# Split expert weights in DRAM rows of 2 KB, and two scratch places for the activations of a transformer layer's expert stage

## The chip, the cores and the metric

One Trainium2 chip, one NeuronCore of it. The metric is the device time of one execution in microseconds, the median of several; the profile is one more execution. The five engines named below are TensorE (PE in the profile; PEld are its weight loads), VectorE (DVE), ScalarE (ACT), GpSimd (POOL) and SyncE (SP). SP, ACT and GpSimd also issue DMAs, each into a queue of its own: q1 is SP's, q10 ACT's, q0 GpSimd's. All queues are served by the same 16 DMA engines of the core.

## The reference

A layer with adaptive normalization on x of 2 x 4096 tokens and 512 channels. The first half is a linear attention, the second a mixture of 8 experts, of which each token takes 2:

```python
h = _layernorm(x) * (1 + ca) + sa
x = x + ga * _L0_attn_ref(h, w_qkv, w_proj, b_proj)
h = _layernorm(x) * (1 + cb) + sb
x = x + gb * _L0_ffn_ref(h, router_logits, gating_einsum, linear, per_expert_scale, router_scale)
# in _L0_ffn_ref, with the tokens sorted by expert:
gate_out = jax.lax.ragged_dot(sorted_xs, w_gate, group_sizes=tokens_per_expert)    # 512 -> 2 x 512
activation = jax.nn.gelu(gate_out[:, 0, :]) * gate_out[:, 1, :]
expert_outputs = jax.lax.ragged_dot(activation, linear, group_sizes=tokens_per_expert)  # 512 -> 512
```

The experts' sizes follow from the router and differ.

## The kernel before, in words

Every fp32 product is computed as three products of split operands: a = hi + lo, each rounded to fp32r, and hi x hi + hi x lo + lo x hi (PASSES).

**Attention stage, groups of 512 tokens, 16 groups.** Beside it the expert weights are split, since they are needed in that form later: SP loads them raw, ACT makes hi, DVE and GpSimd make lo, and SP stores both parts to a DRAM tensor, expert_split (`store_expert`, 64 stores of 768 KB, the only writes to it). An expert has 6144 weights per partition; they are kept as four quarters of QW = 1536, each as hi and lo. Before the change, a DRAM row of expert_split is one partition's hi and lo of one quarter, 3072 floats = 12 KB; a store writes half of it, 6 KB.

**Routing stage, 16 groups.** Projection, second norm, router, and a scatter of every token's row (528 floats) into the lists of its two experts in expert_rows, by indirect DMAs of GpSimd. Before its last group SP already loads the gate and up weights of expert 0 (`early_weights`), the down weights after it.

**Expert stage, 135 items.** An item is 128 rows of one expert's list. The program walks through them in loops of four items, and the expert of an item is read from a table at run time. Per item:

- SP loads the rows into one of four buffers xrow (`load_rows`, four DMAs of 64 KB in rows of 512 B, and meta), when the item four before has been turned.
- DVE transposes them (`turn_x`), ACT and DVE split them into x_t_hi and x_t_lo (`x_hi`, `x_lo`).
- PE computes gate and up, 24 matmuls of 128 x 512; then the down product of the item two before, 12 matmuls. So PE's order is gate(i), up(i), down(i-2).
- ACT applies gelu (gact), DVE multiplies with up (hact).
- hact must be transposed. ACT stores it to a DRAM scratch tensor, act_rows (`store_act`, 128 rows of 2 KB), waits until the store has landed, and loads it back in another order (`act_back`, four DMAs of 64 KB in rows of 512 B, into arow). DVE transposes blocks of arow (`turn_act`), and ACT and DVE split that into act_t_hi and act_t_lo for the down product.
- ACT and DVE make the scale of the output rows (gb, gbr), DVE the output rows orow, and GpSimd adds them to the output by an indirect DMA with accumulation (out_rows).

ACT's order in an item is act_hi(i-2), act_back(i-1), gelu(i), x_hi(i+1), store_act(i), gb_rows(i-2). An engine stands at a wait with all that is behind it. There is one scratch place, so store_act(i) waits for s_ar, that is, until the rows of item i-1 are back. DVE's order is cur_of(i-1), act_lo(i-2), turn_x(i+1), glu(i), x_lo(i+1), turn_act(i-1), out_rows(i-2).

**Weights.** wbuf in SBUF holds two experts, 48 KB per partition each. When an expert's first item has come up, SP asks for the weights of the next one (`next_weights`, `load_weights`): the gate and up part (4 MB, parts 0 to 2 in GATE_UP) once the last up product of the expert before is done, the down part (2 MB, parts 3 and 4 in DOWNS) one item later. They go into SP's queue, in which the x rows are as well. Part 2 is the gate-and-up share of the third quarter, part 3 the down share of it. PE waits for a whole part by s_wg and s_wd. In the first items the weights of expert 1 are loaded too, both parts at once.

Of the kernel before, what the change touches and what calls it, by code (L numbers as in the profile page):

```python
# [28 lines left out]
F32 = mybir.dt.float32  # L29
# [8 lines left out]
P = 128  # L38
B, S, C = 2, 4096, 512
E, H = 8, 512  # L40
HEAD = 32
NT = B * S
FC = C // P
GT = 512
TPG = GT // P
NG = NT // GT
# [6 lines left out]
EW = FC * 2 * H + (H // P) * C  # L53
# [14 lines left out]
AHEAD = 3  # L68
GATE_UP, DOWNS = (0, 1, 2), (3, 4)
EARLY = 3  # L70
# [39 lines left out]
def build(nc, x, c_t, wmod, wqkv, wproj, b_proj, r_w, r_scale, pes, moe_w, out):  # L110
    qd = nc.dram_tensor("q_rows", (NG * P, FC * GT), F32, kind="Internal").ap()
    wd = nc.dram_tensor("expert_split", (E * QPE * P, 2 * QW), F32, kind="Internal").ap()
    mod_d = nc.dram_tensor("mod_rows", (B, 4 * C), F32, kind="Internal").ap()
    xs = nc.dram_tensor("expert_rows", (E * CAP + P, ROW), F32, kind="Internal").ap()
    ad = nc.dram_tensor("act_rows", (P, H), F32, kind="Internal").ap()

# [135 lines left out]
    def f32(ap):  # L252

        return ap.bitcast(F32)
# [153 lines left out]
    def _(sp):  # L408
# [38 lines left out]
        def store_expert(g, s):  # L447
            sp.wait_ge(s_elo, 2 * g + s + 1)
            for k in range(2):
                sp.dma_start(wd[bass.ds((2 * g + s) * P, P), k * QW:(k + 1) * QW], f32(sp_hl[k][:, :])).then_inc(s_wst, 16)  # L450

# [68 lines left out]
        def load_weights(e, half, n):  # L520

            whole, gu = 2 * QW, (FC * 2 * H) % QW
            if n in (0, 1, 4):
                q = min(n, QPE - 1)
                to = wbuf[:, bass.ds(half * 2 * EW + q * whole, whole)]
                of = wd[bass.ds((e * QPE + q) * P, P), :]
            else:
                at, width = ((0, gu), (gu, QW - gu))[n - 2]
                to = wbuf[:, bass.ds(half * 2 * EW + 2 * whole, whole)].rearrange("p (k w) -> p k w", k=2)[:, :, at:at + width]
                of = wd[bass.ds((e * QPE + 2) * P, P), :].rearrange("p (k w) -> p k w", k=2)[:, :, at:at + width]  # L530
            sp.dma_start(f32(to), of).then_inc(s_wg if n in GATE_UP else s_wd, 16)  # L531

        def early_weights():

            sp.wait_ge(s_on, HG * NG)
            for n in GATE_UP:
                sp.wait_ge(s_x1, TPG * (NG - 1) + n)
                load_weights(0, 0, n)
# [249 lines left out]
    def _(act):  # L788
# [237 lines left out]

        def store_act(i):
            wait_apart(act, s_ar, 16 * NBLK * i)
            wait_apart(act, s_h, i + 1)
            act.dma_start(ad[:, :], hact[:, :]).then_inc(s_hst, 16)  # L1030

        def act_back(i):
            wait_apart(act, s_ht, i)
            wait_apart(act, s_hst, 16 * (i + 1))
            for b in range(NBLK):
                act.dma_start(arow[b * BLK:(b + 1) * BLK, :].rearrange("i (a n) -> i a n", a=NBLK),  # L1036
                              ad[:, b * P:(b + 1) * P].rearrange("(a i) n -> i a n", a=NBLK)).then_inc(s_ar, 16)

# [13 lines left out]
        x_hi(1, 1)  # L1052
        store_act(0)

        def item(i, at):
            more = not isinstance(i, int) or i < ITEMS - 1
            lagging = not isinstance(i, int) or i > 1
            if lagging:
                act_hi(i - 2)
            act_back(i - 1)  # L1060
            gelu(i)
            if more:
                x_hi(i + 1, at + 1)
            store_act(i)
            if lagging:
                gb_rows(i - 2, at)

        run_items(act, item)
        act_hi(ITEMS - 2)
        act_back(ITEMS - 1)  # L1070
        gb_rows(ITEMS - 2, ITEMS - 2)
# [1053 lines left out]
```

## Time and profile before

| | us |
|---|---|
| median of 3 runs | 2353.63 (2351.82 to 2355.19) |
| the profiled execution | 2373.91 |
| its span | 2372.1 |
| PE busy | 2165.7 (91%) |
| DVE busy | 1451.2 (61%) |
| ACT, POOL busy | 774.5 (33%), 892.8 (38%) |

By the span's 40 slices, PE's busy tenths are 7999999999888888886499998999989879989997: about 9 in the attention stage (to some 640 us), 8 in the routing stage, 4 to 6 at the passage, 9 with dips in the expert stage (from 1149.7). The whole execution moves 404.88 MB in 292800 packets. A stretch's "granted clock" is the mean share of TensorE's full clock, 1.00 being 2.4 GHz and 0.50 being 1.2 GHz; "DMA share" the mean busy share of the 16 DMA engines. Times in rows count from the span's start. In a row of waits, the engine that waits stands left of the arrow, the instruction that ended the wait right of it.

### The profile page before, as it was taken

The numbers are of one execution on the slowest core, as the hardware profiler recorded it, in microseconds if no ns is written. First come the engines' busy times: TensorE is split into PE (matmuls) and PEld (weight loads), VectorE is DVE, ScalarE is ACT, GpSimd is POOL, SyncE is SP. The second block draws the span as 40 slices with busy tenths as digits, with TensorE's granted clock in tenths as the row PEclk, the third lists the DMA queues.
The fourth block names the chain that finished last, engine by engine and source line by source line (L and its number), as shares of the span: only waits on it lengthen the run. The fifth ranks groups of instructions, "written<-read, shape, count | busy, mean of one in ns | idle before, by whom it ended". The sixth has DMA issues, their size and how long they took to land.

```text
span 2372.1 us, 43953 instructions
## 1 busy us (share of the span) xinstructions
PE 2165.7 (91%) x9280; PEld 1646.8 (69%) x9281; DVE 1451.2 (61%) x3341; ACT 774.5 (33%) x1395; POOL 892.8 (38%) x684
## 2 busy tenths in 40 slices
PE   7999999999888888886499998999989879989997
PEld 5688878888554445554388886887768768868886
DVE  6555555555488888887266664665646536656664
ACT  3244444444333333342123332332223213222332
POOL 5476665665256566675211111111111111111211
PEclk9999999999998899998799998999989989999998
DMA  7565555565444344556655556567676686575564
GB/s 236 206 228 191 205 170 202 165 212 189 160 143 167 137 180 175 182 204 241 220 130 129 130 132 204 125 129 185 154 206 130 166 248 131 128 216 127 129 130 85
DMA packets 292800, 404.88 MB, mean 171 GB/s; under 512 B 50126, under 2 KB 188366, under 8 KB 284878
## 3 DMA queue, kind: packets, MB, share of 16 engines
q1 hardware_dynamic: 164720, 257.57, 33.6%
q0 software_dynamic: 30640, 74.29, 15.4%
q10 hardware_dynamic: 97200, 70.82, 9.3%
q14 instruction: 211, 1.73, 0.2%
q8 instruction: 29, 0.48, 0.1%
HBM read 210.57 MB, written 191.98 MB: 170 GB/s over the span
## 4 chain that ended last, share of the span: by engine, by line
PE 29%; SPq 10%; issue 7%; DMA 5%; DVE 1%; ACTq 1%; ACT 0%; POOL 0%; DVEq 0%
PE bank L1800 29%; SPq L553 3%; DMA arow<-act_rows 3%; SPq L559 2%; SPq L560 2%; DMA act_rows<-hact 1%; SPq L551 1%; SPq L555 1%; DMA wbuf<-expert_split 1%; ACTq L1036 0%; SPq L531 0%; SPq L563 0%; SPq L562 0%; DVE gbr L1725 0%; ACT gb L1048 0%
## 5 line engine op out<-in xcount | busy, mean ns | idle before, releaser
L1800 PE MATMUL bank<-wbuf,x_t_hi 128*128 x2160 | 680.2, 397 | 63.7 <-DVE x_t_lo L1683 52.3
L779 POOL DMA_INDIRECT out_rows<-orow,cur_tok x135 | 209.0, 1548 | 1014.0 <-DVE orow L1728 944.9
L1800 PEld LDWEIGHTS bank<-wbuf,x_t_hi 128*128 128x128 f32 x2160 | 411.2, 191 | 160.6 <-issue 68.0
L1800 PE MATMUL bank<-wbuf,x_t_lo 128*128 x1080 | 427.6, 396 | 0.0
L1800 PE MATMUL bank<-wbuf,act_t_hi 128*128 x1080 | 347.2, 404 | 35.9 <-DVE act_t_lo L1700 18.0
L1689 DVE TENSOR_TENSOR hact<-bank,gact 128x512 f32<-128x512 f32 x135 | 93.3, 691 | 331.7 <-PE bank L1800 300.9
L1800 PEld LDWEIGHTS bank<-wbuf,act_t_hi 128*128 128x128 f32 x1080 | 209.2, 195 | 87.5 <-issue 40.4
L1800 PEld LDWEIGHTS bank<-wbuf,x_t_lo 128*128 128x128 f32 x1080 | 206.1, 191 | 43.5
L1800 PE MATMUL bank<-wbuf,act_t_lo 128*128 x540 | 217.8, 403 | 0.0
L1025 ACT ACTIVATE gact<-bank 128x512 f32<-128x512 f32 x135 | 80.7, 598 | 348.2 <-issue 215.3
L742 POOL DMA_INDIRECT expert_rows<-rows,dest x128 | 133.2, 1040 | 120.3 <-issue 65.0
L1020 ACT ACTIVATE x_t_hi<-bank 128x512 fp32r<-128x512 f32 x135 | 80.8, 599 | 275.2 <-PE bank L1800 260.9
L1048 ACT ACTIVATE gb<-modbc,in_b 128x512 f32<-128x512 f32 x135 | 97.7, 724 | 155.8 <-DVE hact L1689 88.6
L1125 DVE TENSOR_SCALAR hf<-bank,modcol 128x128 f32<-128x128 f32 x256 | 87.3, 403 | 93.9 <-PE bank L1780 93.8
L644 POOL TENSOR_TENSOR k_lo<-k_f,k_hi 128x512 fp32r<-128x512 f32 x64 | 89.1, 1391 | 123.5 <-ACT k_hi L831 123.1
L1695 DVE STREAM_TRANSPOSE bank<-arow 128x512 f32<-128x512 f32 x135 | 96.9, 718 | 50.5 <-DMA arow<-act_rows 50.3
L1725 DVE SCALAR_TENSOR_TENSOR gbr<-modbc,in_b,gb 128x512 f32<-128x512 f32 x135 | 101.5, 752 | 39.7 <-ACT gb L1048 38.0
L1800 PEld LDWEIGHTS bank<-wbuf,act_t_lo 128*128 128x128 f32 x540 | 105.0, 194 | 22.5
L640 POOL TENSOR_TENSOR z_lo<-xg,z_hi 128x512 fp32r<-128x512 f32 x64 | 83.4, 1305 | 97.0 <-ACT z_hi L820 97.0
L1728 DVE SCALAR_TENSOR_TENSOR orow<-bank,cur_w,gbr 128x512 f32<-128x512 f32 x135 | 101.3, 751 | 28.6 <-PE bank L1800 15.1
L1677 DVE STREAM_TRANSPOSE bank<-xrow 128x512 f32<-128x512 f32 x135 | 96.9, 718 | 35.7 <-DMA meta<-expert_rows 35.7
L1800 PE MATMUL bank<-kvp_hi,on_hi 128*128 (+1 forms) x256 | 114.0, 445 | 4.5 <-DVE on_lo L1591 3.6
(225 smaller groups left out, 4125.5 us busy)
## 6 DMA issues: line engine op xcount, KB each, us to landing
wbuf<-expert_split SPq DMA_DIRECT2D x24, 1536.0 KB
xrow<-expert_rows SPq DMA_DIRECT2D x540, 64.0 KB
act_rows<-hact ACTq DMA_DIRECT2D x135, 256.0 KB
arow<-act_rows ACTq DMA_DIRECT2D x540, 64.0 KB
expert_split<-split_hi SPq DMA_DIRECT2D x32, 768.0 KB, 3.5
expert_split<-split_lo SPq DMA_DIRECT2D x32, 768.0 KB, 5.8
xg<-in_x SPq DMA_DIRECT2D x16, 1024.0 KB, 5.4
q_rows<-qf SPq DMA_DIRECT2D x16, 1024.0 KB, 6.7
```

The source lines that it names most:

```text
L640: pool.tensor_tensor(z_hl[1][:, t, :], xg[:, t, :], f32(z_hl[0][:, t, :]), ALU.subtract).then_inc(s_zlo, 1)
L644: pool.tensor_tensor(k_hl[t % 2][1][:, :], k_f[t % 2][:, :], f32(k_hl[t % 2][0][:, :]), ALU.subtract).then_inc(s_klo, 1)
L742: pool.indirect_dma_start(out=xs, out_offset=bass.IndirectOffsetOnAxis(dest[par][:, k, t:t + 1], 0), in_=rows[par][:, t, :], in_offset=Non ...
L779: pool.indirect_dma_start(out=out, out_offset=bass.IndirectOffsetOnAxis(cur_tok[at][:, 0:1], 0), in_=orow[at % 2][:, :], in_offset=None, c ...
L1048: act.activation(gb0[:, :], modbc[:, 0, 3, :], ACT.Copy, scale=in_b0[at % 2][:, 0:1]).then_inc(s_gb0, 1)
L1125: last = ts(hf[t % 2][:, f, :], T_B[t % 2][:, f * P:(f + 1) * P], modcol[:, FC * B + at:FC * B + at + 1], modcol[:, at:at + 1], ALU.mult, ...
L1677: dve.transpose(XT_B[at % 2][:, :].rearrange("c (f a i) -> c a f i", f=FC, a=NBLK), xrow[at][:, :].rearrange("i (a f c) -> i a f c", a=NBL ...
L1689: tt(hact[:, :], U_B[:, :], gact[:, :], ALU.mult).then_inc(s_h, 1)
L1695: dve.transpose(HT_B[:, :].rearrange("c (f a i) -> c a f i", f=FC, a=NBLK), arow[:, :].rearrange("i (a f c) -> i a f c", a=NBLK, f=FC)).th ...
L1725: gbs.did(stt(gbr[:, :], modbc[:, 1, 3, :], in_b1[at % 2][:, 0:1], gb0[:, :], ALU.mult, ALU.add))
L1728: stt(orow[at % 2][:, :], O_B[:, :], cur_w[at % 2][:, 0:1], gbr[:, :], ALU.mult, ALU.mult).then_inc(s_or, 1)
L1800: last = mm(dst, stationary(a, f), moving(b, f), start=(k == 0), stop=(k == parts * n - 1))
```

## The change

expert_split gets rows of UNIT = 512 floats, 2 KB. One part (hi or lo) of a quarter is now three blocks of 128 such rows, one block per 512 columns (PER_PIECE = 3); the rows of one partition lie 128 rows, 256 KB, apart. The stores write 384 rows of 2 KB in place of 128 of 6 KB, the loads of whole quarters read 768 rows of 2 KB in place of 128 of 12 KB. Part 2 of the loads, which was one DMA of 128 x 2 rows of 4 KB, becomes two DMAs (hi and lo) of 128 x 2 rows of 2 KB, so that gate and up have four parts and the down parts are 4 and 5. What lies where in SBUF is the same. act_rows gets two places of 128 rows, used in turn, and the store of item i waits for the rows of item i-2 instead of i-1.

```diff
-GATE_UP, DOWNS = (0, 1, 2), (3, 4)
+GATE_UP, DOWNS = (0, 1, 2, 3), (4, 5)
...
-    wd = nc.dram_tensor("expert_split", (E * QPE * P, 2 * QW), F32, kind="Internal").ap()
+    wd = nc.dram_tensor("expert_split", (E * QPE * 2 * PER_PIECE * P, UNIT), F32, kind="Internal").ap()
...
-    ad = nc.dram_tensor("act_rows", (P, H), F32, kind="Internal").ap()
+    ad = nc.dram_tensor("act_rows", (2 * P, H), F32, kind="Internal").ap()
...
-                sp.dma_start(wd[bass.ds((2 * g + s) * P, P), k * QW:(k + 1) * QW], f32(sp_hl[k][:, :])).then_inc(s_wst, 16)
+                sp.dma_start(wd[bass.ds(((2 * g + s) * 2 + k) * PER_PIECE * P, PER_PIECE * P), :].rearrange("(u p) n -> p u n", p=P),
+                             f32(sp_hl[k][:, :]).rearrange("p (u n) -> p u n", n=UNIT)).then_inc(s_wst, 16)
...
-            whole, gu = 2 * QW, (FC * 2 * H) % QW
-            if n in (0, 1, 4):
-                q = min(n, QPE - 1)
-                to = wbuf[:, bass.ds(half * 2 * EW + q * whole, whole)]
-                of = wd[bass.ds((e * QPE + q) * P, P), :]
+            q, k, units = ((0, 0, 2 * PER_PIECE), (1, 0, 2 * PER_PIECE), (2, 0, PER_PIECE - 1), (2, 1, PER_PIECE - 1),
+                           (2, 0, 0), (3, 0, 2 * PER_PIECE))[n]
+            at = (e * QPE + q) * 2 * PER_PIECE * P
+            if units:
+                to = wbuf[:, bass.ds(half * 2 * EW + (2 * q + k) * QW, units * UNIT)].rearrange("p (u n) -> p u n", n=UNIT)
+                of = wd[bass.ds(at + k * PER_PIECE * P, units * P), :].rearrange("(u p) n -> p u n", p=P)
             else:
-                at, width = ((0, gu), (gu, QW - gu))[n - 2]
-                to = wbuf[:, bass.ds(half * 2 * EW + 2 * whole, whole)].rearrange("p (k w) -> p k w", k=2)[:, :, at:at + width]
-                of = wd[bass.ds((e * QPE + 2) * P, P), :].rearrange("p (k w) -> p k w", k=2)[:, :, at:at + width]
+                to = wbuf[:, bass.ds(half * 2 * EW + 2 * q * QW, 2 * QW)].rearrange("p (k w) -> p k w", k=2)[:, :, QW - UNIT:QW]
+                of = wd[bass.ds(at, 2 * PER_PIECE * P), :].rearrange("(k u p) n -> p k u n", k=2, u=PER_PIECE)[:, :, PER_PIECE - 1, :]
...
             for n in GATE_UP:
-                sp.wait_ge(s_x1, TPG * (NG - 1) + n)
+                sp.wait_ge(s_x1, TPG * (NG - 1) + min(n, 2))
...
-        def store_act(i):
-            wait_apart(act, s_ar, 16 * NBLK * i)
+        def store_act(i, at):
+            wait_apart(act, s_ar, 16 * NBLK * (i - 1))
             wait_apart(act, s_h, i + 1)
-            act.dma_start(ad[:, :], hact[:, :]).then_inc(s_hst, 16)
+            act.dma_start(ad[at % 2 * P:(at % 2 + 1) * P, :], hact[:, :]).then_inc(s_hst, 16)
...
-                              ad[:, b * P:(b + 1) * P].rearrange("(a i) n -> i a n", a=NBLK)).then_inc(s_ar, 16)
+                              ad[at % 2 * P:(at % 2 + 1) * P, b * P:(b + 1) * P].rearrange("(a i) n -> i a n", a=NBLK)).then_inc(s_ar, 16)
```

No compute instruction moves on any engine. On SP, the loads of expert 1's weights, which stand ahead of the loop over the items, read before (name of the SBUF tensor, of the DRAM tensor, shape of the SBUF side):

```order
L555 DMA meta<-expert_rows 128x12
L531 DMA wbuf<-expert_split 128x3072 [waits down_weights_loaded,gate_up_weights_loaded]
L531 DMA wbuf<-expert_split 128x3072
L531 DMA wbuf<-expert_split 128x2x1024
L531 DMA wbuf<-expert_split 128x2x512
L531 DMA wbuf<-expert_split 128x3072
```

and now:

```order
L556 DMA meta<-expert_rows 128x12
L532 DMA wbuf<-expert_split 128x6x512 [waits down_weights_loaded,gate_up_weights_loaded]
L532 DMA wbuf<-expert_split 128x6x512
L532 DMA wbuf<-expert_split 128x2x512 x3
L532 DMA wbuf<-expert_split 128x6x512
```

Whole quarters are cut into six runs of 512 floats per partition, and the DMA of 128x2x1024 has become two of 128x2x512, which stand with the third of that shape (x3). The inside of the loop differs in the same way.

## Rows read from the trace of the kernel before

**Rows 1.** Stretches, PE alone: stretch, length, PE busy (matmuls), clock, DMA share, GB/s.

```profile
1149.00:1200.00 51.00, 39.71 (x151) 0.87 0.70 208
1200.00:1400.00 200.00, 200.00 (x876) 1.00 0.59 130
1446.00:1496.00 50.00, 40.68 (x155) 0.86 0.73 222
1642.00:1692.00 50.00, 43.47 (x175) 0.93 0.79 227
1730.00:1780.00 50.00, 41.12 (x160) 0.86 0.71 216
1884.00:1914.00 30.00, 18.65 (x75) 0.83 0.89 290
1914.00:1960.00 46.00, 38.11 (x152) 0.89 0.77 229
2072.00:2117.00 45.00, 37.48 (x148) 0.92 0.79 243
```

**Rows 2.** Waits of PE, ACT, DVE, 1446 to 2120: total us, times, longest.

```profile
PE bank L1800 <- DMA wbuf<-expert_split: 18.7, 3, 11.3
...
ACT gb L1048 <- DMA arow<-act_rows: 60.7, 13, 10.2
...
DVE bank L1695 <- DMA arow<-act_rows: 42.9, 9, 8.8
...
DVE bank L1677 <- DMA meta<-expert_rows: 18.0, 3, 10.1
```

**Rows 3.** Chain of waits in the expert stage: start us, us, what.

```profile
1149.71 8.38 PE bank L1800 x24
...
1446.86 2.44 DMA act_rows<-hact
...
1450.70 12.14 DMA arow<-act_rows
1463.02 9.52 DMA act_rows<-hact
...
2085.31 5.69 DMA act_rows<-hact
...
2092.40 7.34 DMA arow<-act_rows
```

**Rows 4.** DMA queues, 1453 to 1456: packets, MB, share of 16 engines.

```profile
q1 hardware_dynamic: 101, 1.14, 91.5%
q10 hardware_dynamic: 95, 0.05, 6.1%
```

**Rows 5.** DMA queues, 1107 to 1108.

```profile
q1 hardware_dynamic: 199, 0.41, 104.5%
```

**Rows 6.** DMA queues, 1925.3 to 1927.3.

```profile
q1 hardware_dynamic: 172, 0.70, 89.4%
q10 hardware_dynamic: 169, 0.08, 13.7%
```

**Rows 7.** Timeline of DVE, 1438 to 1482: start us, us, instruction, idle before.

```profile
1451.17 0.72 DVE L1677 STREAM_TRANSPOSE bank<-xrow 128x512 f32<-128x512 f32 x1
...
1462.87 0.73 DVE L1695 STREAM_TRANSPOSE bank<-arow 128x512 f32<-128x512 f32 x1 [7.26 <-DMA arow<-act_rows]
...
1467.19 0.72 DVE L1677 STREAM_TRANSPOSE bank<-xrow 128x512 f32<-128x512 f32 x1
```

**Rows 8.** DMA queues, 1200 to 1400.

```profile
q1 hardware_dynamic: 17664, 6.56, 14.8%
```

**Rows 9.** Timeline of SP, 1445 to 1480.

```profile
1450.15 2.42 SPq L531 DMA_DIRECT2D wbuf<-expert_split  x3
1455.10 2.07 SPq L553 DMA_DIRECT2D xrow<-expert_rows  x4
```

**Rows 10.** Waits for DMAs, 44 to 620.

```profile
DVE st L1098 <- DMA xg<-in_x: 28.7, 12, 2.6
```

More of the change, by code:

```diff
@@ L1025, in gelu, with act_back @@
             act.activation(gact[:, :], G_B[:, :], ACT.Gelu_apprx_tanh).then_inc(s_ga, 1)
-        def store_act(i):
-            wait_apart(act, s_ar, 16 * NBLK * i)
+        def store_act(i, at):
+            wait_apart(act, s_ar, 16 * NBLK * (i - 1))
             wait_apart(act, s_h, i + 1)
-            act.dma_start(ad[:, :], hact[:, :]).then_inc(s_hst, 16)
-        def act_back(i):
+            act.dma_start(ad[at % 2 * P:(at % 2 + 1) * P, :], hact[:, :]).then_inc(s_hst, 16)
+        def act_back(i, at):
             wait_apart(act, s_ht, i)
@@ L1052, in _ @@
         x_hi(1, 1)
-        store_act(0)
+        store_act(0, 0)
         def item(i, at):
@@ L1059, in item @@
                 act_hi(i - 2)
-            act_back(i - 1)
+            act_back(i - 1, at - 1)
             gelu(i)
@@ L1063, in item @@
                 x_hi(i + 1, at + 1)
-            store_act(i)
+            store_act(i, at)
             if lagging:
@@ L1069, in _ @@
         act_hi(ITEMS - 2)
-        act_back(ITEMS - 1)
+        act_back(ITEMS - 1, ITEMS - 1)
         gb_rows(ITEMS - 2, ITEMS - 2)
```

## The prediction, made before the changed kernel ran

> **What bounds the kernel now.** I read the table of stretches first [rows 1]. In the expert stage an undisturbed stretch of 200 us holds 876 matmuls and no idle time at a granted clock of 1.00, so a matmul costs 200 / 876 = 0.2284 us and an item of 36 matmuls 8.22 us: TensorE is the bound there, and what only speeds up its neighbours gains nothing. The other rows of [rows 1] are the stretches in which an expert's weights arrive. What each loses is its length less its matmuls times 0.2284: 50 - 155 x 0.2284 = 14.6 us at 1446, 10.0 at 1642, 13.5 at 1730, 11.3 at 1914, 11.2 at 2072, together 60.6 us. The stretch at 1884 loses 12.9 us, and the first, 1149 to 1200, loses 16.5. These losses hold idle time and slow clock together (granted 0.83 to 0.93: after each stall a part of the time at 1.2 instead of 2.4 GHz).
>
> Then I asked who waits [rows 2]. PE's longest wait, 11.3 us, is for the weights themselves: an expert with one item, whose successor's weights were asked for only when it began. That is the stretch at 1884. Everywhere else the waits start with the activations' trip through DRAM: DVE waits for the rows that come back (42.9 us in 9 waits), ACT's gb waits behind the store that waits for the same rows (60.7 us in 13). The chain of waits gives the trip itself [rows 3]: the store lands in 2.44 us when nothing else runs; under weights it took 9.52 us and the way back 12.14 us.
>
> Why: in 3 us of such a stretch SP's queue moved 101 packets with 1.14 MB (11.3 KB each, so rows of 12 KB) and ACT's queue 95 packets of 0.5 KB [rows 4]. I read this as an engine taking one row from each queue in turn, whatever its length. SP's 101 took 91.5% of 16 engines for 3 us, 0.43 us each. The way back has 4 x 128 rows of 512 B, 32 per engine; 32 x 0.43 = 13.9 us, and 12.14 was seen.
>
> **The change: weights in rows of 2 KB.** Each turn of the weights becomes a sixth. Does the stream get slower? A stream of 2 KB rows alone moved 199 in 1 us, 0.41 MB, 0.08 us per row and engine [rows 5]; the 12 KB rows moved 1.14 MB in 3 x 0.915 us, 0.415 MB/us. So no loss on the stream itself is in the sum; what mixing may cost is a rival below. That turns stay one for one with shorter rows is seen where the weights came in rows of 4 KB: 172 packets against 169 in 2 us [rows 6].
>
> The store has 128 rows, 8 per engine. Now it is 2.44 + 8 x 0.43 = 5.9 us by sharing alone, but 9.52 was seen: 3.6 us are something else that a loaded DMA costs. The new store is 2.44 + 8 x 0.08 = 3.1 plus that 0 to 3.6, so 3.1 to 6.7 us; I take 5.5, near the 5.69 us that a store took at 2085, where mostly 4 KB and shorter rows ran [rows 3]. No row isolates the way back alone and unloaded; I start it at the store's 2.44, add 32 x 0.08 = 2.6 and the same 0 to 3.6: 5.0 to 8.6, taken 6.5, below the 7.34 us at 2092 [rows 3].
>
> The Trainium skill (HBM Reference, section Latency) puts an access at 0.2 us on average and 2 us at high load, which would be 1.8 of the unexplained 3.6 us and would not shrink with the rows; by it the store would be 4.9 us, and with its price on both transfers the forecast would move by less than 5 us. It is a reason against expecting the trip to get as short as sharing alone says; the trace agrees that something beside sharing is there, and shows more than the rule gives.
>
> Does a shorter trip still stall? The loop over two items: store 5.5, issue of the way back about 1.4, way back 6.5, then on DVE from the transposition to the end of the next turn of x rows 1467.19 + 0.72 - 1462.87 = 5.0 us [rows 7], then hact and the issue, 0.8. Sum 19.2, against two items of 8.22 = 16.4: 2.8 us late per two items. Now 9.52 + 1.4 + 12.14 + 5.8 = 28.9 less 16.4 gives 12.5 late per two items, which is the size of the losses above. An expert's 6.3 MB take 6.3 / (0.41 x 0.56) = 27 us at full speed of TensorE, 3.3 items, 1.7 pairs, because the DMA engines are 59% busy without weights [rows 1] and SP's own x rows are 14.8 of these [rows 8], which leaves SP 56%. So 1.7 x 2.8 = 4.7 us of lateness, of which about 1 us is spare before gate: 3.6, and 0.4 for slow clock. **I leave 4 us in each of the five stretches (bounds 0 and 7.2).** Unloaded the same sum is 2.4 + 1.4 + 2.4 + 5.8 = 12, 4.4 us spare, so steady items gain nothing.
>
> **What is late next** are the x rows. They are issued on SP's queue behind the weights. Rows issued at 1455.10, after weights issued at 1450.15 [rows 9], are turned two items after 1451.17 [rows 7], at 1467.6. SP's work up to them is 4.2 MB / 0.41 = 10.2 us and 1.2 of rows (14.8% of an item); at 56% that is done 0.7 + 11.4 / 0.56 us after the issue, at 1471.2, with some 3 us of spare before TensorE (x_t_hi and hact then wait for PE about 2, x_t_lo 1): 0.6 late. The next rows lie behind the down weights too: 17.7 us of SP's work and three items of the others' 44%, 10.9 us, land at 1479.5 against 1475.8 + 3 of spare, so 1 us. If the others take 44% of the whole time it is 3.9. Already now DVE waits 18.0 us in 3 waits for such rows [rows 2]. These stalls fall on the same items as the loop's, so they are in the 4 us at their low value.
>
> **Two places for the scratch rows.** The store no longer waits until the rows before it are back; it is issued as soon as hact is there. ACT's gb, which follows it, stood up to 10.2 us for this [rows 2]. No instruction is added. Queued behind it on ACT are gb, act_t_hi and the issue of the next way back, which all come earlier. With rows of 2 KB the way back (6.5 + 1.4 from its issue) would just fit into an item, so most of its worth goes to the same 60.6 us and isn't counted twice.
>
> **One more DMA for gate and up** (four instead of three, issue about 0.4 us on SP, 8 times): SP has slack in the ring of four; nothing. **The stores in the attention stage** get 2 KB rows: 50 MB at the same rate. DVE waits there for x at most 2.6 us in 12 waits [rows 10], while PE's slices read 8 and 9 at the top of the page; bound 0 to +5 us, taken 0. The early weights end long before GpSimd's scatters, which set the start of the expert stage; nothing.
>
> **The one-item expert stays**: 12.9 us. Its 4.2 MB now let the other queues in more often; packets moved ahead of it are at most an item's out rows and store, so +1 us (bounds 0, +3), and +2 us because two experts' loads follow each other there.
>
> **The first stretch** loses 16.5 us, of which slow clock at the very start is 2.9 (24 matmuls in 8.38 us [rows 3] instead of 5.5) and the filling of the pipeline, by my estimate from x_t_hi's and x_t_lo's 0.6 to 0.7 us with their handovers, two waits of 1.9: 9.8 remain, of which 2 stay.
>
> Sum: 60.6 + 9.8 - 5 x 4 - 2 - 1 - 2 = 45.4 us gained. Profiled execution: 2373.9 - 45.4 = 2328.5 us (its span was 2372.1). The median without profiling is 2353.6, 20.3 lower; I take the same difference off: **2308 us**.
>
> **Rivals.**
> - *All of it is hidden*: transfers start without the unexplained 3.6 us once no long rows are ahead of them. The loop is then 3.1 + 1.4 + 5.0 + 5.8 = 15.3, under 16.4. Gain 66 to 70, time 2284 to 2290. For it: the 3.6 us were seen only behind long rows mostly. Against: the 5.69 us. 17%.
> - *The x rows take over as the bound*: 3.9 + 0.7 us stalls per load, times 60.6 / 40.1 (the loss in the five stretches over their length less PE's busy time [rows 1]) = 7 us, five times, and 10 at the start and the double load: gain 25, 2328 us. For it: 18.0 us of such waits already. Against: a late item stops the others' traffic too. 20%.
> - *Mixed 2 KB rows are slow*, the one that ends slower: if reads of 2 KB beside stores and accumulating out rows take 0.13 us instead of 0.08, SP's work per expert grows from 16 to 25 us, x rows come 3.9 + 9 = 13 us late, less 3 of spare, times 1.5 = 15 us for each of five, and 10 more at the one-item expert: 85 lost against 70 won, 2369 us. It decides from about 0.12 us per row. Against: 199 rows per us. 4%.
> - *The change does not do what it says*: turns are counted in something other than rows, so short rows are sent several to a turn and the trip stays near 20 us; only the second scratch place helps, 5 us or less: 2349 us. Against: 172 to 169. 4%.
>
> **Numbers.** The forecast (2296 to 2320) has 55%, the rivals 17, 20, 4 and 4. The range 2288 to 2328 leaves out the best part of the first rival, the upper part of the second and the last two. A difference under 0.2% (4.7 us) can't be told from none here. Faster: 55 + 17 + 20 and half of the last, 94%; same: the other half, 2%; slower 4%.
>
> **What would show it.** Right: the longest trips under weights are under 9 us; packets of the two queues still count one for one in a loaded us, with ACT's at over 80 per us; the stretches of five loads lose 2 to 6 us each; PE's wait for weights stays 10 to 14 us; the undisturbed stretch still has 876 matmuls in 200 us. Wrong: DVE's waits for x rows grow beyond 30 us, or SP's queue moves less than 0.3 MB in a loaded us, or the attention stage gets longer.

## The result, and the profile after

| | before | after |
|---|---|---|
| median, us | 2353.63 (2346.97 to 2355.19, 5 runs) | 2362.61 (2360.71 to 2363.79, 5 runs) |
| profiled execution, us | 2373.91 | 2362.54 |
| expert stage, first gate matmul to last down product | 1214.0 | 1226.9 |

The ratio is 1.0043, 95% interval 1.0028 to 1.0058: 0.4% slower, where 2308 us had been forecast and 2328 was the top of the range. The two profiled executions mislead if their totals are compared: the one of before reached the expert stage 23.9 us later (at 1149.7, against 1125.8 after), and the expert stage itself became 12.9 us longer. How far two profiles of one kernel differ is seen from the changed kernel, which was profiled once more (e14): its stage took 1231.9 us there. A difference of 5 us between the stages of two profiled executions therefore says little by itself.

The stretches with arriving weights, PE alone (stretch, length, PE busy, clock, DMA share, GB/s), answer to [rows 1]:

```profile
1125.00:1176.00 51.00, 42.03 (x157) 0.88 0.76 218
1200.00:1400.00 200.00, 200.00 (x875) 1.00 0.60 130
1429.00:1479.00 50.00, 42.80 (x177) 0.97 0.81 229
1626.00:1676.00 50.00, 42.07 (x171) 0.93 0.75 200
1715.00:1765.00 50.00, 33.47 (x130) 0.83 0.66 185
1871.00:1901.00 30.00, 16.34 (x63) 0.77 0.94 285
1901.00:1955.00 54.00, 43.92 (x178) 0.94 0.75 210
2065.00:2110.00 45.00, 35.50 (x148) 0.89 0.83 236
```

By the same working (length less matmuls times 0.2284) the five stretches lose 9.6, 10.9, 20.3, 13.3 and 11.2 us: 65.3, where 60.6 were lost before and 20 forecast. The one-item expert loses 15.6 us (12.9 before), the start 15.1 (16.5). Another 7 us are lost where nothing was lost before, between the stretches: 147 us from 1479 to 1626 hold 632 matmuls and 39 us from 1676 to 1715 hold 152, by the same working 2.7 and 4.3 us.

The waits between 1429 and 2105 (total, times, longest) show what changed hands [rows 2]:

```profile
DVE bank L1678 <- DMA meta<-expert_rows: 83.0, 14, 12.8
PE bank L1801 <- DVE x_t_lo L1684: 43.1, 9, 10.1
DVE bank L1696 <- DMA arow<-act_rows: 26.0, 7, 7.1
PE bank L1801 <- DMA wbuf<-expert_split: 17.5, 3, 13.7
ACT gb L1049 <- DMA arow<-act_rows: 3.0, 4, 0.7
```

The waits for the activations' rows fell from 42.9 and 60.7 us to 26.0 and 3.0. Vector's waits for the x rows (named by meta, which is issued last) rose from 18.0 to 83.0 us. The trip is shorter, if less than forecast: in the chain of waits the stores under weights take 6.04 and 7.58 us (9.52 before) and the way back 9.92 (12.14) [rows 3].

```profile
1429.77 6.04 DMA act_rows<-hact
...
1439.41 7.58 DMA act_rows<-hact
...
1448.44 9.92 DMA arow<-act_rows
```

All stores of the stage together show it too: the longest took 8.3 us to land, and 10.9 in e1 below, which has long rows.

The weights' own stream did not suffer. SP's queue from 1720 to 1723, alone (packets, MB, share of 16 engines), moves 206 rows and 0.40 MB per us, as in [rows 5]:

```profile
q1 hardware_dynamic: 617, 1.21, 104.8%
```

Beside the activations' rows, from 1452 to 1454, the packets of the two queues still count one for one, and ACT's are now 149 per us instead of 32 [rows 4]. This is the part of the prediction's mechanism that came true. From 1450 to 1452, where the same mixing has begun and SP's rows are all of 2 KB, they cost 0.09 us each on their engine (93.7% of 16 engines for 2 us over 327 rows), against 0.08 alone. The lines are of 1452 to 1454:

```profile
q1 hardware_dynamic: 293, 0.50, 79.9%
q10 hardware_dynamic: 298, 0.14, 27.7%
```

So why are the x rows late? The timeline of SP (start, us, engine, line) shows how long it takes to issue the weights. Four DMAs took 4.78 and 6.13 us, in the six loads of the loop 2.42 to 6.54; three took 2.42 before [rows 9], and 1.9 to 2.0 in the other five loads:

```profile
1429.40 4.78 SPq L532 DMA_DIRECT2D wbuf<-expert_split  x4
...
1708.52 6.13 SPq L532 DMA_DIRECT2D wbuf<-expert_split  x4
```

And the chain of waits from 1715 to 1730, just ahead of Vector's longest wait there, holds no wait for data. It is SP's own program: two stretches of 5 us in which SP runs no instruction ("issue"), one at the jump back of its loop and one a few instructions behind it, then the issue of the x rows:

```profile
1716.31 5.22 issue
1721.84 5.11 issue
1727.80 0.36 SPq L554
1728.34 0.33 SPq L554
1728.86 0.32 SPq L554
1729.36 0.32 SPq L554
1729.85 0.36 SPq L556
```

A quiet stretch, without weights, shows the same engine at its limit. The x rows of four items in a row, from 1496.10 to 1530.31, are issued in 34.2 us; TensorE needs 4 x 8.22 = 32.9:

```profile
1496.10 1.82 SPq L554 DMA_DIRECT2D xrow<-expert_rows  x4
...
1530.31 1.83 SPq L554 DMA_DIRECT2D xrow<-expert_rows  x4
```

The kernel before was already close to it, and its page said so. Part 4 of the page (the chain that ended last) reads, of before:

```profile
PE 29%; SPq 10%; issue 7%; DMA 5%; DVE 1%; ACTq 1%; ACT 0%; POOL 0%; DVEq 0%
```

and after:

```profile
PE 27%; SPq 13%; issue 9%; DMA 2%; DVE 1%; ACTq 0%; ACT 0%; POOL 0%; DVEq 0%
```

A tenth of the span lay on SP's sequencer and another 7% on "issue" before anything was changed; the prediction never used that line. The second witness is SP's own waits in the expert stage. An engine with time to spare waits for somebody; before it was

```profile
SPq L321 <- DVE in_b L1715: 35.7, 17, 11.2
```

35.7 us in 1214, and after

```profile
SPq L321 <- DVE in_b L1716: 1.2, 1, 1.2
```

### The profile page after: what moved, and what is told of

Read it like the earlier page. It is cut to its first block, busy times and chain, and to the rows that moved or that the text cites. A ratio compares the mean times of both kernels' runs of the same rounds, so it can differ in the third digit from the quotient of the medians.

```text
span 2360.7 us, 43978 instructions
## 1 busy us (share of the span) xinstructions
PE 2152.7 (91%) x9280; PEld 1641.9 (70%) x9281; DVE 1443.6 (61%) x3341; ACT 776.6 (33%) x1395; POOL 893.3 (38%) x684
## 3 DMA queue, kind: packets, MB, share of 16 engines
q1 hardware_dynamic: 198640, 257.57, 34.7%
## 4 chain that ended last, share of the span: by engine, by line
PE 27%; SPq 13%; issue 9%; DMA 2%; DVE 1%; ACTq 0%; ACT 0%; POOL 0%; DVEq 0%
PE bank L1801 27%; SPq L554 4%; SPq L560 2%; SPq L561 2%; SPq L532 1%; SPq L552 1%; SPq L556 1%; DMA act_rows<-hact 1%; DMA arow<-act_rows 1%; DMA meta<-expert_rows 1%; ACTq L1037 0%; SPq L564 0%; SPq L567 0%; SPq L562 0%; SPq L563 0%
## 5 line engine op out<-in xcount | busy, mean ns | idle before, releaser
L1801 PE MATMUL bank<-wbuf,act_t_hi 128*128 x1080 | 341.3, 398 | 19.1 <-DVE act_t_lo L1701 14.1
L1801 PEld LDWEIGHTS bank<-wbuf,act_t_hi 128*128 128x128 f32 x1080 | 205.0, 190 | 67.0 <-issue 22.8
L1043 ACT ACTIVATE act_t_hi<-bank 128x512 fp32r<-128x512 f32 x135 | 81.0, 600 | 127.0 <-PE bank L1801 84.6
L1726 DVE SCALAR_TENSOR_TENSOR gbr<-modbc,in_b,gb 128x512 f32<-128x512 f32 x135 | 101.1, 749 | 28.6 <-ACT gb L1049 27.4
```

What stands on the lines that cost most here:

```text
L1726: gbs.did(stt(gbr[:, :], modbc[:, 1, 3, :], in_b1[at % 2][:, 0:1], gb0[:, :], ALU.mult, ALU.add))
L1801: last = mm(dst, stationary(a, f), moving(b, f), start=(k == 0), stop=(k == parts * n - 1))
```

## The experiments

The theory that grew out of this: **SP's own time is the bound of the x rows.** Its instruction records, summed over four items without weights, give about 33.5 us before and 33.7 after: 20 DMA issues 6.6 us, 20 table reads 6.7, gaps at the jumps 5.2, and some 135 register, branch and semaphore instructions with their spacing the rest. TensorE needs 32.9 us for the four items, so what SP loses at a load of weights it doesn't win back.

All runs in one table. "x rows" is Vector's waiting for x rows in the expert stage, "chain" the share of SPq and of issue in part 4 of the page, "SP, 4 items" SP's time without its waits for four items between loads, the median over the stage after 1480 us. The stage, the waits and the chain are those of one profiled execution each, and the changed kernel's two (after and e14) are 5 us apart in the stage and 21.5 in the x rows. The ratio comes from all runs and is to the kernel before on the same chip. (The figures of 101 and 36 us in the expectations count one more wait, ahead of the first gate matmul. Times in us in the expectations are for a chip on which before takes 2353.6 us; a ratio times that compares with them.)

| kernel | rows, KB | places | SP, 4 items | x rows, us | chain, % | stage, us | ratio (95%) |
|---|---|---|---|---|---|---|---|
| before | 12, 6, 4 | 1 | 33.5 | 19.4 | 10, 7 | 1214.0 | 1 |
| after | 2 | 2 | 33.7 | 87.7 | 13, 9 | 1226.9 | 1.0043 (1.0028 to 1.0058) |
| e1 | 12, 6, 4 | 2 | 33.7 | 22.8 | 7, 6 | 1202.4 | 0.9961 (0.9942 to 0.9979) |
| e2 | 2 | 1 | 34.0 | 73.6 | 22, 15 | 1230.5 | 1.0057 (1.0035 to 1.0079) |
| e3 | 2, early x rows | 2 | 34.7 | 3.4, meta 142.8 | 24, 14 | 1246.6 | 1.0126 (1.0101 to 1.0151) |
| e4 | 12, early x rows | 1 | 31.3 | 3.9, meta 1.1 | 0, 1 | 1209.9 | 0.9948 (0.9924 to 0.9972) |
| e5 | 2, lean SP | 2 | 26.7 | 16.1 | 2, 2 | 1174.3 | 0.9834 (0.9812 to 0.9857) |
| e6 | 12, lean SP | 2 | 25.8 | 4.9 | 0, 1 | 1197.4 | 0.9908 (0.9889 to 0.9926) |
| e7 | 6 | 2 | 33.5 | 48.9 | 17, 12 | 1202.5 | 0.9935 (0.9918 to 0.9952) |
| e8 | 12, busy SP | 2 | 39.9 | 458.1 | 33, 17 | 1367.3 | 1.0672 (1.0651 to 1.0693) |
| e9 | 6, lean SP | 2 | 25.9 | 3.2 | 0, 1 | 1190.6 | 0.9905 (0.9873 to 0.9937) |
| e10 | 2, lean SP | 1 | 26.9 | 9.0 | 1, 2 | 1203.4 | 0.9960 (0.9939 to 0.9981) |
| e11 | 2, loop of eight | 2 | 31.3 | 28.6 | 4, 4 | 1188.7 | 0.9862 (0.9829 to 0.9894) |
| e12 | 2, lean and loop of eight | 2 | 24.3 | 10.4 | 1, 2 | 1179.3 | 0.9830 (0.9794 to 0.9865) |
| e13 | 12, slow issue | 2 | 33.3 | 86.0 | 19, 14 | 1222.4 | 1.0030 (1.0011 to 1.0050) |
| e14 | 2 (after again) | 2 | 34.2 | 109.2 | 18, 12 | 1231.9 | 1.0045 (1.0024 to 1.0066) |

### e1 and e2: each half of the change alone

e1 is the kernel before with the part of the diff that touches act_rows, store_act and act_back; e2 is the changed kernel without that part.

> The kernel before with only the second scratch place for act_rows; expert_split keeps its rows of 12 and 6 KB. Theory A (the short rows do the harm: SP's x rows and SP's own issue come late) expects this part to help a little, since ACT no longer stands behind the rows that come back: 2340 to 2352 us, no x-row waits of DVE beyond the 36 us of before. Theory B (the second place does the harm, since stores now go out into a loaded DMA) expects it to be slower than before by the whole difference, 2360 us or more.

> The changed kernel with one scratch place again, so only the rows of 2 KB. Theory A expects 2360 to 2372 us, as slow as the changed kernel or a little slower, with some 100 us of waits of DVE for x rows in the expert stage. Theory B expects it faster than before, 2310 to 2345 us, since the trip of the activations is short and nothing is against it.

The second scratch place alone made the kernel 0.4% faster, the short rows alone 0.6% slower. So the short rows do the harm, and with them the x rows' waits (22.8 against 87.7 us, 19.4 against 73.6).

### e3 and e4: x rows issued ahead of their meta

```diff
             if not isinstance(i, int) or i >= RING:
                 wait_apart(sp, s_xt, i - RING + 1)
-                wait_apart(sp, s_cur, 2 * (i - RING + 1))
...
+        def load_meta(i, at):
+            if not isinstance(i, int) or i >= RING:
+                wait_apart(sp, s_cur, 2 * (i - RING + 1))
+            r = sp.value_load(tables[0:1, 0, bass.ds(i, 1)], min_val=0, max_val=E * CAP)
+            sp.dma_start(meta[at][:, :], xs[bass.ds(r, P), W_AT:W_AT + META]).then_inc(s_mt[at], 16)
...
         def step(i, at):
             load_rows(i, at)
+            load_meta(i - 2, (at - 2) % RING)
             weights_of(i - AHEAD)
```

> The changed kernel, with the four x-row DMAs of an item issued as soon as the item four before has been turned, some two items earlier; the small meta DMA keeps its place and gets a semaphore of its own. Costs SP one more table read per item, about 0.6 us. Theory A (the x rows, issued and landed too late, are the bound) expects the waits of DVE for x rows to fall from 101 us to under 30 and the time to 2310 to 2335 us. If it was the weights themselves or the activations' trip that got slower, nothing is gained: 2355 us or more.

> The same earlier x rows in the kernel before the change. There the long rows of the weights hold back the activations' trip, and DVE waits for x rows 36 us in the expert stage. Theory A expects a small gain, 2335 to 2352 us, clearly less than the same edit gives the changed kernel. If both kernels gain the same, the short rows have nothing to do with the x rows.

e3 missed: what was gained for the x rows was lost for the meta behind them, 142.8 us in 47 waits, and the kernel became slower still. The edit brings one table read more for each item, and that was the hint: not an order but an amount of work was the trouble. e4 got the same edit and got faster, where less than in the changed kernel had been expected of it. That looked like a contradiction until SP's time was summed. In e4 the gaps at the jumps of the loop are missing (0.4 us for four items, 5.2 in before), so that SP needs 31.3 us in spite of four more reads and gets ahead.

What the gaps are can be read from a queue that carries only instructions, q14 ("instruction"). From 1200 to 2300, before and e4:

```profile
q14 instruction: 157, 1.29, 0.4%
...
q14 instruction: 5, 0.04, 0.0%
```

In before, in the changed kernel and in e3 every one of SP's gaps over 1 us in the stage that aren't a wait (61, 62 and 30 of them) has a packet of this queue in it; e4 has no such gap. By this the gaps are SP waiting for its own code, and in e4 the code of the loop is hardly fetched again. Why it stays loaded in this program and not in e3, whose loop is almost the same, the traces don't show.

### e5 and e6: a lean step of SP

```diff
-            e = sp.value_load(tables[0:1, 1, bass.ds(i, 1)], min_val=0, max_val=E - 1)
             of_e = sp.value_load(tables[0:1, 2, bass.ds(i, 1)], min_val=0, max_val=ITEMS)
-            with sp.If(e > 0):
-                with sp.If(e < E - 1):
-                    with sp.If(of_e < 1):
+            with sp.If(of_e < 1):
+                e = sp.value_load(tables[0:1, 1, bass.ds(i, 1)], min_val=0, max_val=E - 1)
+                with sp.If(e > 0):
+                    with sp.If(e < E - 1):
```

> The changed kernel, in which SP reads of an item only its place in its expert, and the expert's number inside the branch that is taken where an expert begins: two table reads and up to four branches less for each item, some 0.9 us of a step of SP, nothing else is changed. Theory (SP's own time is the bound of the x rows: its loop of four items takes 34.0 us in the changed kernel where TensorE takes 32.9, and the blocked issue of the short-row weights puts 3 to 9 us on top at each load, which is never won back): the loop falls to about 30 to 31 us, SP is ahead again a few items after each load, Vector's waits for x rows fall from 101 to 20 to 40 us, the expert stage from 1227 to 1185 to 1200 us; ratio to before 0.975 to 0.988. Rival (the x rows are late because they stand behind the weights' rows in SP's DMA queue, whatever SP does): waits stay at 75 to 100 us, stage 1220 to 1230, ratio 1.000 to 1.006.

> The kernel before with two scratch places and the same lean SP step as in the run before this: weights in rows of 6 and 12 KB. Theory (SP's time): the loop of four items falls from 33.0 to 34.3 us to 30 to 31, Vector's waits for x rows from 23 us to under 10, the waits for the activations' rows stay at 50 to 60 us since the long rows stay, stage 1202 to about 1190 to 1198; ratio to before 0.985 to 0.993. Rival (SP irrelevant): as with two places alone, 0.994 to 0.998.

In e5 SP reads of each item only its place in its expert, and the expert's number only where an expert begins. This decides that SP's time was the bound. Without a single change in what is loaded, computed or queued, the changed kernel goes from 1.0043 to 0.9834. SP needs 26.7 us for four items (30 to 31 expected; the x rows' waits, 16.1 us, and the stage, 1174.3, are also below what was expected) and waits again, in the expert stage of e5

```profile
SPq L321 <- DVE in_b L1716: 137.8, 72, 3.2
```

and in part 4 of e5's page the chain is TensorE's:

```profile
PE 40%; DMA 5%; issue 2%; SPq 2%; DVE 1%; POOL 0%; ACTq 0%; ACT 0%; DVEq 0%; POOLq 0%
```

The gate and up weights of e5 still land 17.7 to 18.7 us after their issue began (17.8 to 19.4 in the changed kernel, 15.6 to 16.6 in e6 with long rows), and the x rows still stand behind them in the queue; the issue of gate and up still takes up to 5.9 us. Its stretches (columns as before) are what the prediction had in mind:

```profile
1123.00:1174.00 51.00, 43.06 (x162) 0.87 0.79 223
...
1420.00:1470.00 50.00, 45.54 (x187) 0.97 0.83 232
1600.00:1650.00 50.00, 47.06 (x203) 1.00 0.86 239
1679.00:1729.00 50.00, 45.18 (x183) 0.93 0.80 229
1829.00:1859.00 30.00, 25.23 (x102) 0.89 1.04 312
1859.00:1905.00 46.00, 41.32 (x171) 0.96 0.86 240
2009.00:2054.00 45.00, 42.51 (x176) 0.96 0.90 255
```

The five lose 7.3, 3.6, 8.2, 6.9 and 4.8 us, 30.8 in all; the one-item expert loses 6.7, the start 14.0. e6, long rows with the lean step, reached 0.9908. Its x-row waits fell to 4.9 us as expected, but Vector's waits for the activations' rows are 95.2 us where 50 to 60 were expected: once the x rows are in time, the trip under long rows is what Vector waits for, and it is 62.8 us in e5. **So what the short rows are worth depends on SP's time.** By the stage, with two places: 24.5 us lost (1202.4 to 1226.9) where SP is full, 23.1 us won (1197.4 to 1174.3) where it is not. By the ratios it is 0.8% lost and 0.7% won.

### e7 and e9: rows of 6 KB

```diff
-    wd = nc.dram_tensor("expert_split", (E * QPE * P, 2 * QW), F32, kind="Internal").ap()
+    wd = nc.dram_tensor("expert_split", (E * QPE * 2 * P, QW), F32, kind="Internal").ap()
...
-                to = wbuf[:, bass.ds(half * 2 * EW + q * whole, whole)]
-                of = wd[bass.ds((e * QPE + q) * P, P), :]
+                to = wbuf[:, bass.ds(half * 2 * EW + q * whole, whole)].rearrange("p (k w) -> p k w", k=2)
+                of = wd[bass.ds((e * QPE + q) * 2 * P, 2 * P), :].rearrange("(k p) w -> p k w", k=2)
```

> The kernel before with two scratch places and the split weights in rows of 6 KB: 256 rows in each of the five loads of an expert where before has 128 rows of 12 KB in three of them; SP's code is otherwise that of before. Theory (the issue of DMAs of many rows blocks SP): 1280 rows for an expert lie between before (896) and the changed kernel (3072), SP's issue time in a loop with a load between 9 and 12 us, x-row waits 20 to 50 us, ratio to before 0.994 to 1.001. If the harm goes simply with the row's length as the DMA engines take turns, the activations' wait for their rows falls from 56 us to about 40 and the x rows' rises by as much, ratio 1.000 to 1.003.

> Weights in rows of 6 KB, two scratch places, SP's lean step. With long rows the lean step made 0.9961 into 0.9908, with short ones 1.0043 into 0.9834. Theory (once SP has time to spare, what is left of the row's length is the activations' wait for their rows alone: 95 us of Vector's time at 12 KB, 63 at 2 KB): waits of 70 to 85 us, x-row waits under 10, ratio to before between the two, 0.984 to 0.990. Rival (6 KB is short enough for the trip and has fewer rows to issue): as good as or better than 2 KB, 0.980 to 0.984.

1280 rows for an expert don't block SP: the issue groups of gate and up take 1.8 to 2.2 us, no more than with 896, where something between that and the changed kernel's had been expected. The stage is as long as with 12 KB rows (1202.5 against 1202.4); the activations' waits fall from 56.4 to 51.2 us and the x rows' rise from 22.8 to 48.9, by a little more than two profiles of one kernel can differ. SP needs no more time here than in e1 (33.5 against 33.7 us for four items), so x rows can come later for another reason than SP's time, and what that reason is was not tested. The ratio, 0.9935, lies at the edge below the expected. With the lean step 6 KB rows gain 7 us of stage on 12 KB and are 16 us behind 2 KB; the ratio, 0.9905, is just above the expected 0.984 to 0.990 and no better than that of 12 KB, and the rival is out. The time does not fall evenly with the row.

### e8: long rows, a busy SP

```diff
             r = sp.value_load(tables[0:1, 0, bass.ds(i, 1)], min_val=0, max_val=E * CAP)
+            for _ in range(3):
+                sp.value_load(tables[0:1, 0, bass.ds(i, 1)], min_val=0, max_val=E * CAP)
```

> The kernel before with two scratch places, long rows, and three more table reads for each item on SP whose result nobody uses: some 0.35 us each with their register operations. Theory (SP's own time): SP's loop of four items goes from 33.0 to 34.3 us to 37 to 38.5 us, over TensorE's 32.9, so SP sets the whole expert stage: 33 loops of some 4 us more give 1202 plus 110 to 150 us, Vector's x-row waits 150 us and more; ratio to before 1.04 to 1.06. Rival (SP has slack, its ring of four covers it): ratio 0.994 to 0.998, as with two places alone.

Three unused table reads for each item made the kernel 6.7% slower, more than expected. SP's four items take 39.9 us, 6.2 more than in e1, and the stage is 165 us longer: 33 times 5.0. Nothing else is the bound there:

```profile
SPq 33%; issue 17%; PE 2%; DMA 2%; DVE 1%; ACT 0%; POOL 0%; ACTq 0%; DVEq 0%
```

### e10: one scratch place, with SP lean

The edit is that of e5 in e2.

> The changed kernel's short rows with one scratch place instead of two, with SP's lean step: what the second place is worth once the x rows are no longer late. The prediction held it to be worth little with short rows. By the waits of the changed kernel and of the one with one place (ACT's wait in front of the store 47 against 203 us, before the gate row 4 against 42 us), much of which is not in TensorE's way: ratio to before 0.983 to 0.990; if the place is worth nothing, 0.9834 as with two; if it is worth what it was with long rows (0.4%), 0.987 or more.

Missed: without the second place the ratio is 0.9960, outside the expected 0.983 to 0.990, where it was 0.9834 with two places, and the stage is 29 us longer (1203.4 against 1174.3). ACT stands 78.3 us in front of gb until the rows before are back (5.7 in e5):

```profile
ACT gb L1049 <- DMA arow<-act_rows: 78.3, 23, 7.8
```

With SP full the place was worth 12 us with long rows (1214.0 to 1202.4); with short ones (1230.5 to 1226.9, ratios 1.0057 and 1.0043) no difference is clear of the scatter. So the gain of e5 needs the second place as well as SP's time; with long rows the place alone won 0.4% without that.

### e11 and e12: SP's loop of eight items

```diff
-        with sp.Fori(0, (ITEMS - RING) // RING) as j:
-            for u in range(RING):
-                step(RING * (j + 1) + u, u)
+        with sp.Fori(0, (ITEMS - RING) // (2 * RING)) as j:
+            for u in range(2 * RING):
+                step(2 * RING * j + RING + u, u % RING)
```

> The changed kernel with SP's loop written out for eight items instead of four and nothing else: the same instructions run in the same order, with half as many jumps back, each of which stands for some 2.5 us (twice that under a load of weights) without an instruction on SP. Theory (SP's time, whatever it is spent on): four items take 34.0 less 1.5 to 2.6 us, 31.5 to 32.5 us on SP, a little under TensorE's 32.9; x-row waits fall from 101 to 40 to 70 us, ratio to before 0.988 to 0.997. If the table reads themselves and not SP's time did the harm, nothing changes: 1.002 to 1.006. If the gaps come elsewhere with the longer code (they were not there in one of the kernels run), also nothing.

> The changed kernel with both: SP's lean step and the loop of eight. Theory (SP was only the bound until it had a few us to spare; then TensorE is): x-row waits from 16 to under 12 us, the rest as with the lean step alone, ratio to before 0.981 to 0.984. Rival (every us of SP's time still counts, at the loads above all): 0.976 to 0.981.

e11 runs the same instructions in the same order as the changed kernel, with half the jumps, and is 1.4% faster than before instead of 0.4% slower, a little better than expected. So it is SP's time, whatever it is spent on. e12 is as fast as e5 within the intervals: once SP has a few us to spare, more of it buys nothing that these runs can show. Its interval, 0.9794 to 0.9865, still reaches into the rival's 0.976 to 0.981.

### e13 and e14: which part of the short rows fills SP

Open was whether the longer issue or the later landing in the queue does the harm. In the six loads inside the loop, the issue of the weights takes 38.8 us of SP in the changed kernel and 19.7 in e1; in the load at the start of the stage it is 8.8 against 2.9, so 25 us more in all. e13 gives long rows extra time of SP in the same places.

```diff
                         for n in parts:
                             load_weights(nxt, nxt & 1, n)
+                        for _ in range(8 if parts is GATE_UP else 0):
+                            sp.value_load(tables[0:1, 2, bass.ds(i, 1)], min_val=0, max_val=ITEMS)
```

> The kernel before with two scratch places and long rows, and eight unused table reads on SP behind the gate and up loads of each expert, some 0.4 us each: 3.2 us in each of six places, 19 us in all. This is the time by which SP's issue of the weights is longer in the changed kernel (38.8 us from the second expert's loads on, 19.7 with long rows and two places). If that time on SP is what made the short rows slower: stage from 1202 to 1218 to 1228 us, Vector's x-row waits from 23 to 60 to 100 us, ratio to before 1.002 to 1.007, as the changed kernel's. Rival (the late x rows come from the queue, in which 3072 short rows take 22 to 27 us to land and the x rows follow): stage 1200 to 1208, waits 20 to 40 us, ratio 0.995 to 0.999.

> The changed kernel once more, beside the other kernel of this call on the same chip: 1.003 to 1.006 times before.

The eight reads took 4.4 to 4.6 us in each of the six places, 26.7 us in all and not the 19 that had been expected, since a read with its register steps took 0.55 us there. The stage lost 20.0 us (1202.4 to 1222.4), and Vector's waits for x rows are the changed kernel's:

```profile
DVE bank L1679 <- DMA meta<-expert_rows: 86.0, 18, 14.9
```

The seven turns of SP's loop in which weights are issued tell the same. Without SP's waits they take 280.8 us in e1, 305.9 in the changed kernel, 306.8 in e14 and 307.2 in e13. So e13 and the changed kernel spend the same time on SP, and by the ratios are nearly as slow.

The changed kernel, on the same chip, came to 1.0045 again. The intervals of the two overlap; whether the remaining 0.15% is the later landing is not settled. Nor is how much of the trip's gain the changed kernel kept: e13 has long rows and loses nearly as much.

## Why the prediction was wrong

**The step that failed** is the term "One more DMA for gate and up": "SP has slack in the ring of four; nothing." It priced only the fourth DMA, at 0.4 us, and set the slack without a row for it. The ring of four is room, not time: an engine that needs 33.5 us where TensorE needs 32.9 doesn't fill it again. And it did not ask what the issue of these DMAs, two of them with 768 rows, costs. Measured: 25 us more of SP's time over the stage. 26.7 us of SP's time, added to long rows, became 20.0 us of the stage (e13), and with SP lean the same short rows won 23.1 us where they had lost 24.5. The page had the warning in part 4, SPq 10% and issue 7%, and SP's 35.7 us of waits in 1214 gave the slack.

**What is late next** named the right successor, the x rows, and the wrong reason. It priced the queue (1 us late, 3.9 at the most) and took SP's issue times as given. The test that it set itself, Vector's x-row waits "beyond 30 us", was met by 83.0. The rival "x rows take over" had this result's form but the price of the queue, 2328 us, and so was still faster than before. The rival that ends slower, mixed 2 KB rows at 0.12 us and more, was not what happened: they cost 0.09 us beside ACT's rows. That the time still came out on that rival's side is by another mechanism.

**The trip** got shorter in the way described, but the sizes were low: stores of 6.0 and 7.6 us (5.5 taken, 3.1 to 6.7 bounded), a way back of 9.9 (6.5, up to 8.6). In e5 they are 5.69, 6.72 and 7.40. Where sharing alone gives 3.1 us for a store, 2.9 and 4.5 us of the two stores are something else, as 3.6 were with long rows; they did not shrink with the rows. The Trainium skill (HBM Reference, section Latency) has an access at 2 us under high load. The trace agrees that a part beside the sharing is there, and shows more than these 2 us. Of the signs that the prediction named, the one-for-one count (293 to 298), PE's wait for the weights (13.7 us) and the undisturbed stretch (875 matmuls) came true, the way back under 9 us and the stretches' 2 to 6 us did not.

**The five stretches**, 4 us left in each: 13.1 on average in the changed kernel; with SP lean 6.2 on average (3.6 to 8.2), about at the upper bound of 7.2. **The one-item expert**, "stays": 15.6 us, as said, in the changed kernel, but 6.7 with SP lean. **The start**, 7.8 us gained: 1.4 measured, 2.5 with SP lean. In sum e5's stage is 39.7 us shorter than before's, against the 45.4 forecast, but the lean step has a part of its own in that: with long rows and two places it made the stage 5.0 us shorter and the ratio 0.5% better (e1 to e6). The kernel before with the lean step alone was not run, so the change's own worth behind the bound isn't measured; the 23.1 us of the short rows (e6 to e5) show that the mechanism was there.

**The second scratch place**, "most of its worth goes to the same 60.6 us": it does serve the same waits, but the prediction put the gain down to the shorter trip. With SP lean, 29 us of e5's 40 are gone without the place (e10), so the short rows alone don't bring them.

**The difference of 20.3 us** between the profiled run and the median was taken off the forecast of the profiled execution, which comes to the same as taking the 45.4 us off the median of before, 2353.6. At least a part of it lay in the routing stage: from 700 to 860 the profiled run of before held 561 matmuls at a granted clock of 0.91, that of after 592 at 0.94. It has no part in the error.

## What to carry to other kernels

Before pricing a transfer, price the engine that issues it: sum its instructions over one turn of its loop, gaps at the jumps included, and compare with the bound's turn; if the page's chain has SPq and issue in it, or the issuer hardly ever waits, it has no slack, however deep the ring of buffers is. A change that only moves DMAs about can then lose what it wins, and two table reads and a few branches less on that engine are worth more than the change (here they turned 0.4% slower into 1.7% faster). When two parts of a change serve the same wait, neither can be judged until the other bound is out of the way.

## What the runs showed of the hardware

- **The issue of a DMA can be held up.** In the changed kernel a load's third and fourth DMA, of 256 rows each behind two of 768, took 1.09 and 1.65 us to issue at 1431 and the fourth up to 4.5 us elsewhere, where such an instruction takes 0.4. In one of the six loads of the loop, at 1617, it took 0.4 as well. With 1280 rows of 6 KB or 896 of up to 12 KB it stayed at 0.3 to 0.7 in the loop. The Trainium skill (DMA: Bandwidth & Descriptors, section Issuing engines are not separate DMA queues) says the time on the sequencer "is usually small relative to the DMA itself"; small it is here too, 6 us beside the 18 until the weights have landed, and yet it set the time.
- **A jump back in SP's loop can cost time, in which its code is fetched by DMA.** Some 2.5 us at the jump and 2 to 3 soon after, about 5.2 us for four items, 9 to 11 while weights arrive. Every such gap has a packet of the instruction queue in it. A loop of eight pays it once for eight items; in one program (e4) the gaps and the packets were both missing.
- **The two queues' rows take turns one for one, whatever their length**: 101 rows of 11.3 KB against 95 of 0.5 KB in 3 us before, 293 of 1.7 KB on average against 298 of 0.5 KB in 2 us after.
- **A table read on SP** takes mostly 0.27 us and at times 0.5 and more, with its register instructions 0.5; in e8 twelve more of them made 6.2 us.
